# A decoder layer on one core: idle stretches of TensorE filled in three stages, and the context rows loaded earlier

## The reference

```python
x = x + attn(layernorm(x))        # 16 heads of 8, causal in windows of 64
x = x + xattn(layernorm(x), ctx)  # keys and values by one of 8 weight sets, chosen by each row's bucket
x = x + ffn(layernorm(x))         # below
# ffn(y): y1 = LN(y + mha(y)); y2 = LN(y1 + moe(y1))
#   mha: 4 heads of 32; each position attends over the 16 sequences of the batch, row by row
#   moe: 8 experts, no nonlinearity between w1 and w2; the best expert by softmax gate,
#        at most 256 rows each, others get zero
```

## Time and profile before

| | |
|---|---|
| median of 3 runs | 341.99 us (337.6 to 343.11) |
| profiled execution | 339.86 us, span 338.1 us |
| PE busy | 317.0 us, 94% of the span |
| DVE, ACT, POOL busy | 261.2, 164.7, 126.8 us |
| mean granted TensorE clock | 0.98 |

### The profile page before, as it was taken

The page is one execution under the profiler, slowest core; times in us unless marked ns, Lnnn a source line. Parts: engine busy times, 40 slices in busy tenths (PEclk is TensorE's granted clock), DMA queues, the critical chain, the costliest instruction groups (busy, mean ns, idle before and its releaser), DMA issues.

```text
span 338.1 us, 12320 instructions
## 1 busy us (share of the span) xinstructions
PE 317.0 (94%) x4772; PEld 217.5 (64%) x4772; DVE 261.2 (77%) x663; ACT 164.7 (49%) x454; POOL 126.8 (38%) x208
## 2 busy tenths in 40 slices
PE   7869999999999999999999999989989999998993
PEld 3435556666666565655656556557567769887992
DVE  6874688866666899989899999856456548869996
ACT  2223546666666455463565646554424438633330
POOL 1074556100000345546224344233700006614896
PEclk9976999999999999999999999999999999999998
DMA  4962230636466174589393000000000000125212
GB/s 118 314 180 84 86 121 28 178 116 161 149 154 156 59 183 124 146 196 249 117 214 103 3 2 2 4 5 0 2 2 4 4 0 2 50 80 189 95 33 63
DMA packets 38698, 31.89 MB, mean 94 GB/s; under 512 B 4969, under 2 KB 36209, under 8 KB 38513
## 3 DMA queue, kind: packets, MB, share of 16 engines
q1 hardware_dynamic: 36064, 27.37, 28.9%
q0 software_dynamic: 1280, 3.15, 3.5%
q10 hardware_dynamic: 1296, 0.59, 0.7%
HBM read 23.40 MB, written 7.70 MB: 92 GB/s over the span
## 4 chain that ended last, share of the span: by engine, by line
PE 78%; DVE 10%; issue 5%; POOL 5%; ACT 1%; POOLq 0%; DVEq 0%
PE ps L1262 10%; PE ps L1299 10%; PE ps L1316 10%; PE ps L1272 4%; PE ps L1228 3%; PE ps L1215 3%; PE ps L1236 3%; PE ps L1387 3%; PE ps L1349 3%; PE ps L1332 2%; PE ps L1206 2%; PE ps L1672 2%; PE ps L1405 2%; PE ps L1425 2%; POOL room L909 2%
## 5 line engine op out<-in xcount | busy, mean ns | idle before, releaser
L965 ACT ACTIVATE pT<-ps 128x512 f32<-128x512 f32 x128 | 73.9, 613 | 88.9 <-PE ps L1272 88.9
L833 POOL TENSOR_TENSOR rstd<-veps,minus_half 128x1 f32<-128x1 f32 x32 | 18.8, 588 | 115.5 <-DVE veps L448 115.4
L483 DVE TENSOR_REDUCE m_pad<-ps 128x8 f32<-128x1024 f32 x32 | 39.1, 1221 | 18.1 <-PE ps L1299 17.9
L459 DVE TENSOR_TENSOR p_sb<-qk_sb,heads 128x512 f32<-128x512 f32 x64 | 45.0, 704 | 0.9 <-ACT qk_sb L980 0.5
L486 DVE TENSOR_REDUCE m_pad<-ps 128x8 f32<-128x1024 f32 x32 | 38.9, 1214 | 0.0
L1262 PE MATMUL ps<-p_sb,qk_sb 32*128 32x512 f32 x256 | 38.1, 667 | 0.0
L1299 PE MATMUL ps<-p_sb,qk_sb 32*128 32x512 f32 x256 | 37.7, 659 | 0.0
L1316 PE MATMUL ps<-pT,p_sb 128*32 128x128 f32 x1024 | 35.3, 275 | 0.0
L1672 PE MATMUL ps<-mexp,pT 128*128 128x128 f32 x256 | 31.9, 278 | 1.7 <-DVE pT L777 1.5
L1272 PE MATMUL ps<-mT,negsel 32*128 32x128 f32 x512 | 32.4, 363 | 0.6 <-issue 0.6
L1672 PEld LDWEIGHTS ps<-mexp,pT 128*128 128x128 f32 x256 | 29.8, 192 | 2.5 <-DVE pT L777 2.3
(11 more groups left out here) (197 smaller groups left out, 677.2 us busy)
## 6 DMA issues: line engine op xcount, KB each, us to landing
room<-mask_rows SPq DMA_DIRECT2D x32, 128.0 KB, 3.7
wkv_sb<-wkv SPq DMA_DIRECT2D x23, 128.0 KB
kv_sorted<-room SPq DMA_DIRECT2D x5, 512.0 KB, 3.2
w1t_sb<-w1t SPq DMA_DIRECT2D x8, 256.0 KB
w_sb<-w SPq DMA_DIRECT2D x8, 256.0 KB
kv_sb<-hot_rows SPq DMA_DIRECT2D x4, 512.0 KB, 4.3
ctx_sorted<-room SPq DMA_DIRECT2D x1, 1472.0 KB, 10.0
tk<-fside SPq DMA_DIRECT2D x1, 1024.0 KB
```

The costliest lines, as they stand in the source:

```text
L459: return dve.tensor_tensor(dst, rows.unsqueeze(1).broadcast_to([128, QUADS, S]), heads[:, 0, :].unsqueeze(2).broadcast_to([128, QUADS, S]) ...
L483: dve.tensor_reduce(m4[:, 0:2, 0:QUADS], ps[:, 0:2, :].rearrange("p g (j k) -> p g j k", j=QUADS), AX.X, ALU.max).then_inc(s["max_low"], 1)
L833: pool.tensor_tensor(rstd[:, :], veps[:, :], minus_half[:, :], ALU.pow)\
L965: act.activation(pT[:, t % 2, g, :, :], quad[4 + g], ACT.Exp).then_inc(s["exped"], 1)
```

## The change

- SP issues the load of the context rows directly behind x 1 to 3, before its waits for the tables.
- The product of expert 0 moves from period T - 1 to T - 2, behind the output projection; that of expert 1 takes its place in T - 1.
- In the last attention, the value product of round 1 moves from round 1 to round 0 (bank 0 instead of bank 4, behind the first maxima), and DVE's addition with it.
- PE leaves `project_and_turn` after m = 19. The turns of blocks 14 and 15 (now in a free part of bank 7) and the logits of blocks 13 to 15 stand between `ffn(0)`, `spread_hot(2)`, `ffn(1)`, `spread_hot(3)` and `ffn(2)`.
- In the last norm, DVE scales rows 12 and 13 after the variance of row 14 and no longer finishes them: ACT multiplies by the root, PE adds them to the residual by two products with the identity each, ACT copies the sums to `y0`. DVE finishes rows 14 and 15 behind both scalings.

```diff
             sp.dma_start(x_sb[:, 1:4, :], x[1:4].rearrange("b s d -> s b d")).then_inc(s["x_more_in"], 16)
+            sp.dma_start(ctx_sb[:, :, :], ctx.rearrange("b s d -> s b d")).then_inc(s["ctx_in"], 16)
             sp.wait_ge(s["heads_in"], 16)
             sp.wait_ge(s["sort_in"], 48)
             sp.wait_ge(s["consts_in"], 32)
-            sp.dma_start(ctx_sb[:, :, :], ctx.rearrange("b s d -> s b d")).then_inc(s["ctx_in"], 16)
...
-                    sp.wait_ge(s["last_rows"], 2)
+                    sp.wait_ge(s["pair_rows"], 2)
...
             for i in range(4):
                 mha_maxima(i)
+                if i == 0:
+                    mha_values(1)
+                if i >= 2:
+                    mha_values(i)
                 if i >= 1:
-                    mha_values(i)
                     mha_outputs(i - 1)
...
-                    if b == B - 3:
-                        for a in (b - 1, b):
-                            z_scaled(a, 1, ln_rows[:, 2, :])
                     if b == B - 2:
                         last_variance(b)
-                        z_scaled(b, 1, ln_rows[:, 2, :])
                         for a in (b - 2, b - 1):
-                            z_rows(a, 1, x_sb[:, a, :], y0, "last_rows")
+                            z_scaled(a, 1, ln_rows[:, 2, :])
...
-            z_rows(B - 2, 1, x_sb[:, B - 2, :], y0, "last_rows")
             last_variance(B - 1)
-            z_scaled(B - 1, 1, ln_rows[:, 2, :])
-            z_rows(B - 1, 1, x_sb[:, B - 1, :], y0, "last_rows")
+            for a in (B - 2, B - 1):
+                z_scaled(a, 1, ln_rows[:, 2, :])
+            for a in (B - 2, B - 1):
+                z_rows(a, 1, x_sb[:, a, :], y0, "last_rows")
...
+            for b in (B - 4, B - 3):
+                act.wait_ge(s["rs_ready"], B + B - 1)
+                act.wait_ge(s["w_ready"], B + b - (B - 4) + 1)
+                act.activation(z16[:, b, :], z16[:, b, :], ACT.Identity, scale=rs16[:, b:b + 1])\
+                   .then_inc(s["u_ready"], 1)
+            for b in (B - 4, B - 3):
+                act.wait_ge(s["pair_summed"], b - (B - 4) + 1)
+                act.copy(y0[:, b, :], bank[b % 2][:, 0:D]).then_inc(s["pair_rows"], 1)
...
-                if p in EXPERT_PERIODS[:2]:
-                    experts(EXPERT_PERIODS.index(p), 0)
+                if p == T - 1:
+                    experts(0, 1)
+                if p == T + 1:
+                    experts(1, 0)
...
+                if p == T - 2:
+                    experts(0, 0)
+                if p == T + 1:
+                    experts(1, 1)
+                if p == T + 3:
+                    experts(2)
...
                 if i == 0:
                     mha_by_key(0)
+                    mha_project_v(1)
+                if i >= 2:
+                    mha_project_v(i)
                 if i >= 1:
-                    mha_project_v(i)
                     mha_weighted(i - 1)
...
-            for m in range(B + 7):
+            for m in range(B + 4):
                 project_and_turn(m)
...
-                if m == 19:
-                    place(0)
-                    ffn(0)
-            for b in range(1, B):
-                if b + 1 < QUADS:
-                    spread_hot(b + 1)
+            place(0)
+            ffn(0)
+            spread_hot(2)
+            row_logits(B - 3)
+            turn_row(B - 2)
+            ffn(1)
+            row_logits(B - 2)
+            turn_row(B - 1)
+            spread_hot(3)
+            row_logits(B - 1)
+            for b in range(2, B):
                 ffn(b)
...
+            for b in (B - 4, B - 3):
+                pe.wait_ge(s["u_ready"], b + 1)
+                pe.matmul(bank[b % 2][:, 0:D], ident[:, :], x_sb[:, b, :], start=True, stop=False)
+                pe.matmul(bank[b % 2][:, 0:D], ident[:, :], z16[:, b, :], start=False, stop=True)\
+                  .then_inc(s["pair_summed"], 1)
```

More of the change, by code:

```diff
@@ L258, in sums_bank, with turned_bank @@
             return 0 if i < 3 else 4
+        def turned_bank(b):
+            return bank[4 + b % 2][:, 0:128] if b < 14 else bank[7][:, 256:384]
         def four_batches(rows, i):
@@ L639, in mha_values @@
                 dve.wait_ge(s["v_done"], i + 1)
-                dve.tensor_tensor(vM[:, 4 * i:4 * i + 4, :], quad[5 if i == 0 else 4],
+                dve.tensor_tensor(vM[:, 4 * i:4 * i + 4, :], quad[(5, 0, 4, 4)[i]],
                                   inb_rows[:, :].unsqueeze(1).broadcast_to([128, QUADS, D]), ALU.add)\
@@ L1109, in turned_row @@
                 act.wait_ge(s["y1T_done"], b + 1)
-                act.activation(y1T[:, b, :], bank[4 + (b % 2 if b < 13 else 1)][:, 0:128], ACT.Identity,
+                act.activation(y1T[:, b, :], turned_bank(b), ACT.Identity,
                                bias=be1_col[:, 0:1]).then_inc(s["y1T_copied"], 1)
@@ L1177, in _ @@
                     by_root(b)
+            for b in (B - 4, B - 3):
[6 more added lines that the diff above has]
+                act.copy(y0[:, b, :], bank[b % 2][:, 0:D]).then_inc(s["pair_rows"], 1)
             for b in (B - 2, B - 1):
-                act.wait_ge(s["last_rows"], b - (B - 4) + 1)
+                act.wait_ge(s["last_rows"], b - (B - 2) + 1)
                 act.dma_start(out[b:b + 1].rearrange("b s d -> s b d"), y0[:, b:b + 1, :]).then_inc(s["stored"], 16)
@@ L1482, in mha_project_v @@
             def mha_project_v(i):
-                if i >= 1:
+                if i == 1:
+                    pe.wait_ge(s["f_max_low"], 1)
+                if i >= 2:
                     pe.wait_ge(s["f_exped"], 4 * i - 3)
                 for r in range(QUADS):
-                    mm = pe.matmul(quad[5 if i == 0 else 4][:, r, :], y0T[:, 4 * i + r, :], inw_sb[:, 2 * D:3 * D],
+                    mm = pe.matmul(quad[(5, 0, 4, 4)[i]][:, r, :], y0T[:, 4 * i + r, :], inw_sb[:, 2 * D:3 * D],
                                    start=True, stop=True)
@@ L1503, in mha_by_query @@
                     pe.wait_ge(s["f_mT_copied"], i)
+                if i == 1:
+                    pe.wait_ge(s["v_ready"], 2)
                 if i >= 2:
@@ L1515, in mha_by_key @@
             def mha_by_key(i):
-                pe.wait_ge(s["v_ready"], i + 1)
+                pe.wait_ge(s["v_ready"], max(i, 1) + (1 if i >= 2 else 0))
                 if i >= 1:
@@ L1593, in _, with turn_row, row_logits @@
             pe.wait_ge(s["aT_ready"], 4)
+            def turn_row(b):
+                if b >= 2:
+                    pe.wait_ge(s["y1T_copied"], b - 1)
+                pe.wait_ge(s["y1_rooted"], b + 1)
+                pe.transpose(turned_bank(b), y1[:, b, :], ident[:, :]).then_inc(s["y1T_done"], 1)
+            def row_logits(b):
+                pe.wait_ge(s["y1T_copied"], b + 1)
+                h, a = divmod(b, B // 2)
+                if b == B // 2:
+                    pe.wait_ge(s["crep_copied"], 1)
+                pe.matmul(bank[6 + h][:, a * E:(a + 1) * E], y1T[:, b, :], wg_sb[:, :], start=True, stop=True)\
+                  .then_inc(s["logits_done"], 1)
             def project_and_turn(m):
@@ L1602, in project_and_turn @@
                       .then_inc(s["f_proj_done"], 1)
-                b = m - 6
-                if 0 <= b < B:
-                    if b >= 2:
-                        pe.wait_ge(s["y1T_copied"], b if b > 13 else b - 1)
-                    pe.wait_ge(s["y1_rooted"], b + 1)
-                    pe.transpose(bank[4 + (b % 2 if b < 13 else 1)][:, 0:128], y1[:, b, :], ident[:, :])\
-                      .then_inc(s["y1T_done"], 1)
-                b = m - 7
-                if 0 <= b < B:
-                    pe.wait_ge(s["y1T_copied"], b + 1)
-                    h, a = divmod(b, B // 2)
-                    if b == B // 2:
-                        pe.wait_ge(s["crep_copied"], 1)
-                    pe.matmul(bank[6 + h][:, a * E:(a + 1) * E], y1T[:, b, :], wg_sb[:, :], start=True, stop=True)\
-                      .then_inc(s["logits_done"], 1)
+                if 0 <= m - 6 < B - 2:
+                    turn_row(m - 6)
+                if 0 <= m - 7 < B - 3:
+                    row_logits(m - 7)
             def turn_picks(h):
@@ L1661, in ffn @@
                 if b < 2:
-                    pe.wait_ge(s["y1T_copied"], 13 if b == 0 else B)
+                    pe.wait_ge(s["y1T_copied"], 13 + b)
                 else:
```

6 lines of the change are left out of this document (1 added, 5 removed).

## The result

| | before | after |
|---|---|---|
| median of 22 runs each | 339.94 us (336.88 to 343.89) | 337.51 us (334.92 to 341.28) |
| profiled execution | 339.86 us, span 338.1 | 336.94 us, span 335.1 |
| mean granted clock of the profiled execution | 0.98 | 0.987 |

The account below looks back on a forecast made before the run. PE was taken to hold most of the chain of waits, often at half clock early on. 339.86 - 0.6 - 0.36 - 1.2 = 337.7, plus 1.07 towards the timed runs' median, gave 338.8 us; range 335.0 to 342.3.

Parts of the forecast that it names:

- since the slots come last: Head: the slots, at 17.79, release the first scatter, so earlier load or zero rows give 0.
- perhaps twice its 2.7: Head: sharing by turns, table `before` takes about double and lands near 8.1 at worst, 1.2 after DVE wants it.
- Tables late: Head rival: tables beside the context load delay DVE if `before` lands after 6.90; full price 3.9, 342.7; chance 0.13.
- The head gains: Head rival: the 0.91 before the scatter and the second slow stretch's 3.4 go, giving 335.4; chance 0.10.
- Two signs that I had given: Head: first scatter at 17.8 plus a little under 1 us; another clock pattern before 31 us would be wrong.
- End of the second pass: First expert half fills PE's 1.14 idle before the score masks: gain 0.6, bounds 0 and 0.9.
- the period starts 0.1 late: End of second pass: ACT's copy of the turned row ends about 0.1 after 224.58, delaying the period by 0.1.
- no idle bracket over 0.3: Sign: at the masks of the last second-pass period, no idle bracket exceeds 0.3.
- Last attention: Round 1's value product fills round 0's 1.06 idle; turn moves from 255.44 to 255.08: gain 0.36, bounds 0 and 1.06.
- Expert stage: Start of expert stage: earlier spread of batch 2, DVE then sets the pace; gain 1.2 at ffn(4), bounds 0.6 and 1.4.
- The rival that POOL swallows the gain: Expert stage to end: POOL may keep its own pace from 318 us, absorbing the 1.2, giving 340.0; chance 0.17.
- a POOL chain without gaps that the change leaves alone: Tail: POOL's power at 334.52 is the last wait and stays; value 0, bounds -0.3 (gain) and +0.5.

Follow-up runs that it names:

- experiment 1: Changed kernel with the context load back behind SP's waits for the tables: 329.91 us against 332.54 before, ratio 0.990.
- experiment 6: Changed kernel with the context load back behind the waits, expert 0's product behind the turned row, batch 3's spread directly behind batch 2's: 330.43 us, ratio 0.9906.
- experiment 7: Kernel before with only the new order of turns, logits and spreads at the start of the expert stage: one run, 334.77 us.
- experiment 2: Kernel before with only the context load moved up: 333.91 us, ratio 1.0016.
- experiment 5: Changed kernel with expert 0's product in period T - 2 behind the turned row instead of ahead of it: 330.93 us, ratio 0.9931.
- experiment 11: Changed kernel with the context load back behind the waits and expert 0's product behind the turned row: 329.97 us, ratio 0.9884.
- Experiment 8: Kernel before with only the tail's part, rows 12 and 13 finished by ACT and PE: one run, 333.61 us.
- Experiment 10: Changed kernel plus one 128x512 DVE product near the end, in two kernels: both operands in SBUF, 330.78 us; one in PSUM, 330.6 us.
- experiment 9: Kernel before with only the last attention's part, the second-round value product moved up: one run, 332.85 us.

## Why the prediction was right, and where its terms were off

**Head: right in its value, for one wrong reason.** It took 0 "since the slots come last". In the changed kernel's profile they don't: SP's next issue was costed at 6.36 + 0.88, as if only the context load had stood between the tables and the zero rows, but its release is the *last* table, and I followed `before` alone. By turns between the queues, weighed as "perhaps twice its 2.7", `before` would have landed near 8.1; it landed at 6.5. The two tables behind it in ACT's queue bear the doubling: the mask takes 6.2 instead of the 2.8 of experiment 1, the identity 6.8 instead of 2.9. The Trainium skill, "DMA: Bandwidth & Descriptors", section on queues, rings and completion order, has each DMA engine take turns between queues with work. The trace agrees, but on other tables than I put it on. PE's new wait of 1.02 did not carry to the slots: they are at 17.28, where they were at 17.62, because PE's faster first projections let DVE go on with the sort some 0.5 us earlier, and the masks lost only 0.03. Nor do the slots come last as a rule with the late load: in experiments 6 and 7 they are there at 17.23, and the zero rows release the scatter, at 18.26 and 18.15. That the value 0 held is in part luck: two errors, the zero rows and the tables, met a margin that varies with the clock.

**The rivals of the head.** *Tables late* would decide once `before` landed after 6.90; it did not, and the 0.54 to 1.40 of PE's wait for the later table did not become the 3.9. *The head gains* looked true in the first profile, with 0.72 us and another grant at 17 to 21. It falls by experiments 1 and 2: the load alone is 1.0016, and the load taken back keeps all of the gain. Yet the clock goes with the load in most profiles: from 0 to 22 us the mean grant is 1.00 in five of the seven profiles with the early load and in none of the seven with the late one (0.91 to 0.98; both counts with the first two profiles); the other two with the early load have 0.84 and 0.92. It buys no time that can be seen; the pause at 10 us and the later scatter stand against it. Two signs that I had given failed, and the forecast held all the same: a different clock pattern before 31 us was there, and the first scatter came 1.2 us after 17.8, not a little under 1.

**End of the second pass: 0.45 instead of 0.6.** Two terms were mis-sized. The first is "the period starts 0.1 late". Beyond the 0.66 that the head brings, the masks would start at 223.92; they start at 224.13, 0.21 late, because ACT's copy of the turned row ends at 223.99 and its handover takes 0.14. (The bracket of 0.45 there also breaks the sign "no idle bracket over 0.3".) The second is the handover behind ACT's exponentials, which were rightly named as the last wait of the weighted sum: they end at 228.81 and the sum starts at 228.92, 0.11 that the forecast had left out. Its 230.03 - 229.37 = 0.66, less 0.11 and 0.11, is 0.44. Putting the half behind the turn gives back the 0.21, in experiments 5 and 11.

**Last attention: 0.28 instead of 0.36.** Mechanism as put: the product fills the pause, and the second maxima set the turn of round 1. The size was off by the handover: I let the turn start 0.04 after the maxima; it starts 0.14 after them (253.93 and 254.07).

**Expert stage: 1.18 for 1.2.** DVE sets the pace from batch 3 on, PE's wait at `ffn(4)` goes from 0.86 to 0.42. DVE's bracket for batch 3 grew instead of shrinking, from 0.70 to 1.27, against what I gave as a sign: beyond the 1.39 of the stages ahead, DVE starts batch 2 earlier by 1.76 and batch 3 by 1.19. My own sum already said so (batch 2 at 296.6 and batch 3 at 299.7 are 3.1 apart, 2.5 before), so the sign was wrong and not the sum. An earlier spread buys only 0.06 (experiment 6), since the buffer is not free and then PE sets the pace. The rival that POOL swallows the gain falls by experiment 7.

**Tail: 0.36 instead of 0.** This is the step that failed: "a POOL chain without gaps that the change leaves alone". The chain ended last and had no gap, as put, but its operations are not of fixed length. Its last subtractions take 0.45 or 0.46 each (0.51 to 0.53 before), and from the start of the last one to the power it is 0.41 us (331.18 to 331.59) instead of 0.55. Experiment 8 shows that the tail's own edit does this. The prediction had the rule for it from the Trainium skill, "SBUF — State Buffer", section on the two separate sides, which calls the port that DVE and POOL share an exclusive lock. It took a bound of -0.3 from it, which the 0.36 exceeds, and the value 0. Experiment 10 agrees with the rule in kind: the operands in SBUF hold POOL. In size it doesn't quite: the product of 0.68 began 0.14 ahead, so by an estimate from these rows a full lock would have held the subtraction 0.54 us, and it was held 0.39; the measurement decides.

How the edit shortens POOL's operations is argued and not shown. Two DVE operations on two SBUF operands fewer run beside them (the last products of rows 12 and 13). But the others also start at another moment, and in the changed kernel it seems to be DVE that waits: its last two scalings take 1.06 us together where those of rows 12 and 13 take 0.82, and the second of them runs beside POOL's last subtraction, which takes no more than its 0.46.

```profile
330.72 1.06 DVE L719 SCALAR_TENSOR_TENSOR room<-room,mv,ln_rows 128x128 f32<-128x128 f32 x2
```

No run separates the fewer operations from the other order.

**The sum.** The parts gave 0.45 + 0.28 + 1.18 + 0.36 = 2.27, against 2.16 forecast and 0.9942 of 340, which is 1.97. The tail's 0.36 makes up for the 0.15 and 0.08 that two stages gave less, so the agreement of the sum is luck, and the head varies by more than any of the misses. The 1.3 us between the forecast of 338.8 and the measured 337.51 come from elsewhere: 1.07 of them are what I added for the median of three runs, 341.99, and 22 runs of the same kernel have 339.94. Two slips in the working changed nothing: the rival of the head takes off the 3.4 but not the 0.91 that it names, and the range, 335.0 to 342.3, ends inside the full price of *Tables late*, 342.7.

## What to carry to other kernels

Before a load is moved ahead of a queue of small ones, write down the landing of every one of them and who waits for the last, not for the one nearest to use. When a pause is filled, put the work behind whatever another engine must still do before the pause ends (here, the turned row that ACT copies), not ahead of it. A stage's gain is best read at the same instructions of two traces, with stretches at another clock taken out.

## What the runs showed of the hardware

- The clock of the first 55 us differs between executions with the same head, on one chip too: experiments 6, 7 and 8 have a grant of 0.92, 0.98 and 0.91 up to 22 us, and 1.00, 0.96 and 0.95 from there to 55. Windows from 0 to 22 and 22 to 55 us, the last columns are the grant, the DMA share and GB/s. Experiment 1, and experiment 9 with the same order of loads:

```profile
0.00:22.00 22.00, 17.60 (x142) 8.77 (x143) 17.39 (x53) 5.03 (x15) 5.06 (x11) 0.92 0.73 207
22.00:55.00 33.00, 32.25 (x584) 19.93 (x584) 27.76 (x60) 19.26 (x54) 21.32 (x22) 1.00 0.39 122
```

```profile
0.00:22.00 22.00, 16.28 (x145) 8.60 (x146) 17.33 (x53) 5.62 (x16) 5.04 (x11) 0.92 0.75 208
22.00:55.00 33.00, 32.46 (x565) 20.09 (x566) 27.13 (x57) 18.90 (x53) 21.09 (x22) 0.95 0.35 115
```

- The same kernel takes 340 us in the first measurement and 333 on the chips of the experiments. Nearly all of the difference is there by the statistics that start at 51.98 in the first profile and some 6 us earlier in the others. The first two profiles have a grant of 0.90 from 22 to 55 us, the others 0.95 to 1.00: up to 3.3 us of full-speed work. 4.2 us of it lie between two statistics instructions of the kernel before (21.96 and 32.16; in experiment 11 21.95 and 27.96), and from 24 to 31 us the grant was 0.51 there and 1.00 in experiment 11. What makes the rest is open.
- A stretch at half clock inside the last attention (experiment 7, behind 246 us) cost 1.5 us between the exponentials of rounds 0 and 1, five times what the change gives there.
